# The last two feed forward layers of a Perceiver kernel: rotation on PSUM tiles, norms last, values behind the keys, token shift inside a projection

## The chip, the core and the metric

One core of one Trainium2 chip runs the whole program in one launch. The metric is the device time of an execution in microseconds (us). The profile is of one execution. TensorE's clock has two levels, 1.2 and 2.4 GHz; the profile gives the granted clock as a share of 2.4 GHz.

## What is computed

The reference is twelve residual blocks on x of 2 x 256 tokens by 256 channels. The change touches the twelfth, `L3_ffn`, which holds two layers (l = 0 and 1) of this form, each an attention with 8 heads of 64 and a gated feed forward:

```python
def _layer(x, wqkv, qs, ksc, wo, lg, lb, w1, b1, w2, b2):
    h = shift_token(x)                 # channels 128 to 255 one token later, per batch
    q, k, v = jnp.split(h @ wqkv, 3, axis=-1)
    q, k, v = (to_heads(q), to_heads(k), to_heads(v))
    q = l2norm(q) * qs                 # one norm per token and head
    k = l2norm(k) * ksc
    q, k = rotary_xpos(q, k)           # q*cos*scale + rotate_half(q)*sin*scale
    o = local_attention(q, k, v)
    x = x + o @ wo
    h = shift_token(x)
    h = layernorm(h) * lg + lb
    a, g = jnp.split(h @ w1 + b1, 2, axis=-1)
    x = x + (a * gelu(g)) @ w2 + b2
    return x
```

The block's own input is the layer norm of x; its output is added to x.

## The kernel before

The program is written out by hand, one function for each block and engine (`l3f_pe(l)`, `l3f_dve(l)`, `l3f_act(l)`, `l3f_pool(l)`, `l3f_sp(l)`), and each engine runs its functions in order. An event recorded with `at(...)` is a semaphore count; `wait_ge(engine, ...)` waits for it. `after(engine, stage)` waits for all engines' ends of a stage. Tokens lie in four tiles of 128 (t = 0 to 3, two of each batch). `banks` hands out the eight PSUM banks in turn; a bank is reused when the events given with `take` have come (`settle`).

A layer goes through these stages. The layer input XN is transposed on TensorE into HT (L289), and the second half of the channels is copied out one column further, which is the token shift (L2399). Queries and keys are projected, n = 0 to 7, four tiles of each, 512 wide (L318 through `tokp_pe`). ScalarE squares every tile into SQ (L2469), VectorE sums the squares by head (L2403). When all eight are there, one root (L2471) and one reciprocal (L2407) follow, and VectorE goes over the eight tiles again: scale by the norm out of PSUM (L2411), times q_scale or k_scale (L2418), the two halves of the turned part (L2424 and L2426, on GpSimd for odd n: L2506 and L2509), times the cosine table (L2434), sum (L2439). TensorE transposes the results (L2364), then projects the values (L318). The attention (`attn_pe` and the others) starts with L415. Its output OT3 goes through the output projection (L318, 16 matmuls of 256 columns) and is added to XN (L330). Then the shifted input XS of the layer norm is made: GpSimd copies the first half of the channels, and SP's queue moves the second half one partition down with two transfers per tile (L2534 to L2538). Statistics (L260, L262), root (L277) and scaling (L267, L269) of the four tiles follow, transposes (L289) and the affine step (L302). The feed forward is 24 matmuls of 512 columns (L310), Gelu (L2489), product (L2456), 24 matmuls of 256 (L318), the addition to XN (L330) and of b2 (L333). In layer 1 X is added (L2462) and stored (L2545). The block ahead, `l3a`, ends with a layer norm by tiles (`addout_dve` with `ln`), and has a fourth operand (L333) in each tile's addition. A ScalarE function table is loaded with `preload_act_table`. An f32 matmul is two records of TensorE in the profile, a transpose one.

## Time and profile before

| | us |
|---|---|
| three runs, median (lowest, highest) | 2343.68 (2337.89, 2343.77) |
| the profiled execution | 2344.69 |
| its span | 2343.4 |
| TensorE busy in the span | 2017.7 (86%) |
| VectorE busy | 1447.3 (62%) |
| ScalarE busy | 1161.7 (50%) |
| GpSimd busy | 555.7 (24%) |

The two layers take the last 290 us of the span: layer 0 from 2053.6, layer 1 from 2197.7. Busy shares are of the whole span; in the rows below the share of a stage is what counts. PE is TensorE, PEld its weight loads, DVE VectorE, ACT ScalarE, POOL GpSimd, SPq the queue of SyncE, PS PSUM, WK, WA and WB large SBUF tensors.

### The profile page before, as it was taken

The numbers are of one execution on the slowest core, as the hardware profiler recorded it, in microseconds if no ns is written. First come the engines' busy times: TensorE is split into PE (matmuls) and PEld (weight loads), VectorE is DVE, ScalarE is ACT, GpSimd is POOL, SyncE is SP. The second block draws the span as 40 slices with busy tenths as digits, with TensorE's granted clock in tenths as the row PEclk, the third lists the DMA queues.
The fourth block names the chain that finished last, engine by engine and source line by source line (L and its number), as shares of the span: only waits on it lengthen the run. The fifth ranks groups of instructions, "written<-read, shape, count | busy, mean of one in ns | idle before, by whom it ended". The sixth has DMA issues, their size and how long they took to land.

```text
span 2343.4 us, 36521 instructions
## 1 busy us (share of the span) xinstructions
PE 2017.7 (86%) x13415; PEld 1185.4 (51%) x13415; DVE 1447.3 (62%) x3518; ACT 1161.7 (50%) x2481; POOL 555.7 (24%) x849
## 2 busy tenths in 40 slices
PE   5999999998985899999998889988876877856776
PEld 2545554444553545554454655475555665624343
DVE  2577667784766377667784655412658994764462
ACT  2466666665433366566675611421527881613131
POOL 3132222213611322122200500000413441512030
PEclk8999999999987999999999989999988999978988
DMA  7455445560021655445541013520031322001100
GB/s 171 92 134 124 111 105 132 116 162 1 1 72 44 108 127 127 107 116 136 122 69 58 18 50 104 160 90 14 1 104 58 100 73 77 2 13 41 44 2 13
DMA packets 122546, 187.25 MB, mean 80 GB/s; under 512 B 22632, under 2 KB 70304, under 8 KB 122016
## 3 DMA queue, kind: packets, MB, share of 16 engines
q1 hardware_dynamic: 122368, 184.92, 31.8%
q8 instruction: 107, 1.75, 0.3%
q14 instruction: 71, 0.58, 0.1%
HBM read 131.86 MB, written 2.13 MB: 57 GB/s over the span
## 4 chain that ended last, share of the span: by engine, by line
PE 68%; DVE 16%; ACT 5%; SPq 4%; issue 2%; POOL 2%; DMA 2%; ACTq 0%; DVEq 0%; POOLq 0%
PE PS L712 9%; PE PS L694 9%; PE PS L663 8%; PE PS L310 7%; PE PS L318 6%; PE PS L630 5%; PE PS L618 4%; DVE WK L2108 3%; SPq L995 3%; PE PS L1637 2%; PE PS L1662 2%; PE PS L415 2%; PE PS L463 2%; PE PS L442 2%; ACT WK L514 2%
## 5 line engine op out<-in xcount | busy, mean ns | idle before, releaser
L768 DVE TENSOR_REDUCE WK<-PS 128x1 f32<-128x1024 f32 x512 | 609.2, 1221 | 310.4 <-PE PS L663 308.3
L874 ACT ACTIVATE WK<-PS 128x512 f32<-128x512 f32 x1024 | 542.0, 600 | 197.2 <-PE PS L694 191.2
L694 PE MATMUL PS<-WK 100*128 100x256 bf16 x2048 | 322.9, 275 | 7.1 <-ACT WK L874 6.4
L663 PE MATMUL PS<-WK 100*128 100x512 bf16 x1024 | 304.9, 381 | 8.7 <-DVE WK L768 3.7
L694 PEld LDWEIGHTS PS<-WK 100*128 100x128 bf16 x2048 | 166.8, 98 | 215.4 <-ACT WK L874 74.7
L712 PE MATMUL PS<-WK 128*32 128x256 f32 x3072 | 207.0, 386 | 0.0
L514 ACT ACTIVATE WK<-PS,WK 128x256 f32<-128x256 f32 (+1 forms) x320 | 140.6, 451 | 74.6 <-DVE WK L482 44.5
L540 POOL TENSOR_TENSOR WK<-WK 128x128 f32<-128x128 f32 (+1 forms) x128 | 65.0, 508 | 370.4 <-DVE WK L500 308.1
L936 POOL TENSOR_SCALAR WK<-WK 128x2 bf16<-128x2 f32 x64 | 12.5, 195 | 570.5 <-DVE WK L774 373.1
L712 PEld LDWEIGHTS PS<-WK 128*32 128x32 f32 x3072 | 80.6, 109 | 112.4 <-issue 78.0
L310 PE MATMUL PS<-HT,WB 128*128 128x512 f32 x248 | 120.8, 646 | 5.6 <-DVE HT L302 1.9
L544 POOL TENSOR_TENSOR WK<-WK 128x512 f32<-128x512 f32 x96 | 100.0, 1041 | 77.2 <-DVE WK L497 59.1
L923 POOL TENSOR_TENSOR WK<-WK 128x512 f32<-128x512 f32 x64 | 74.1, 1157 | 168.1 <-ACT WK L845 89.5
L663 PEld LDWEIGHTS PS<-WK 100*128 100x128 bf16 x1024 | 94.5, 98 | 36.9 <-DVE WK L768 16.2
L415 PE MATMUL PS<-WK 32*128 32x256 f32 (+2 forms) x640 | 85.8, 391 | 13.1 <-ACT WK L514 10.1
L491 DVE COPY WK<-PS 128x512 f32<-128x512 f32 (+1 forms) x144 | 88.3, 619 | 4.7 <-PE PS L442 4.7
L442 PE MATMUL PS<-idf,WK 128*128 128x128 f32 x576 | 84.5, 287 | 4.4 <-DVE WK L491 2.6
L310 PEld LDWEIGHTS PS<-HT,WB 128*128 128x128 f32 x248 | 51.2, 209 | 68.3 <-issue 60.3
L2108 DVE MAX8 WK<-WK 128x8 f32<-128x16 f32 x1088 | 84.5, 161 | 0.0
L442 PEld LDWEIGHTS PS<-idf,WK 128*128 128x128 f32 x576 | 66.7, 146 | 20.4 <-issue 9.3
L318 PE MATMUL PS<-WB,WK 128*128 128x256 f32 x320 | 71.2, 382 | 6.5 <-DVE WK L2456 3.3
L927 POOL TENSOR_TENSOR WK<-WK 128x512 bf16<-128x512 f32 x64 | 74.3, 1161 | 5.3
(334 smaller groups left out, 3303.9 us busy)
## 6 DMA issues: line engine op xcount, KB each, us to landing
WK<-WK SPq DMA_DIRECT2D x768, 64.0 KB
WB<-in_ctxT SPq DMA_DIRECT2D x78, 512.0 KB, 4.8
WK<-in_ctxT SPq DMA_DIRECT2D x40, 512.0 KB, 3.7
WA<-in_ctxT SPq DMA_DIRECT2D x26, 512.0 KB, 4.7
WK<-in_ctx SPq DMA_DIRECT2D x8, 1024.0 KB, 5.6
WK<-in_ctx SPq DMA_DIRECT2D x16, 512.0 KB, 3.9
WK<-scratch_q SPq DMA_DIRECT2D x12, 256.0 KB, 8.3
WB<-in_L3f_qkv SPq DMA_DIRECT2D x2, 1536.0 KB, 6.6
```

Source lines behind the costliest of these rows:

```text
L310: i = pe.e.matmul(b.ap, W[:, k, c0:c0 + 128], rhs[:, k, :], start=k == 0, stop=k == kt - 1)
L318: i = pe.e.matmul(b.ap[:, 0:n], lhs[:, k, t * 128:(t + 1) * 128], W[:, k, c0:c0 + n], start=k == 0, stop=k == kt - 1)
L415: x = pe.e.matmul(two[u].ap[:, c0:c1], qs[:, bb * 256 + q * 128:bb * 256 + (q + 1) * 128], ks[:, bb * 256:bb * 256 + c1 - c0], start=q == ...
L442: x = pe.e.transpose(b.ap[:, c:c + 128], PN[j % 4][:, q * 256 + kk * 128:q * 256 + (kk + 1) * 128], idf[:, :])
L514: ac.e.activation(PP[i % 4][:, c0:c1], tile[tag, "S", i][:, c0:c1], ACT.Exp, bias=r[:, q:q + 1], scale=1.0, accum_out=r[:, 2 + q:3 + q]).t ...
L630: x = pe.e.matmul(b.ap[:, t // 2, t % 2 * 256:t % 2 * 256 + 256], ct[:, k, t * 128:(t + 1) * 128], W["v"][:, k, :], start=k == 0, stop=k == 1)
L663: x = pe.e.matmul(b.ap[:, u, :], QS[0:100, h, bb * 256 + q * 128:bb * 256 + (q + 1) * 128], KS[s % 4][0:100, c * 1024 + u * 512:c * 1024 + ...
L694: x = pe.e.matmul(b.ap[:, j * 256:j * 256 + 256], KS[s % 4][0:100, kt * 128:(kt + 1) * 128], QS[0:100, h, bb * 256:bb * 256 + 256], start= ...
L712: x = pe.e.matmul(pv.ap[32 * j:32 * j + 32, 0:256], V[vbuf[g]][:, kt * 136 + 17 * hh:kt * 136 + 17 * hh + 32], PR[n % NPR][:, kt % 2 * 256 ...
L768: dv.e.tensor_reduce(mt[:, n:n + 1], tile["R", L, s, n].rearrange("p a b -> p (a b)"), AX, ALU.max).then_inc(*dv.at("R", L, s, n))
L874: ac.e.activation(PR[n % NPR], tile["S", L, s, i], ACT.Exp).then_inc(*ac.at("E", L, s, i))
L2108: dv.e.max(m8[:, g, :], n3[:, g, :]).then_inc(*dv.at())
```

## The change

- **Rotation.** The tables of cosine and sine are multiplied with q_scale and k_scale ahead of time, for both layers, on GpSimd in `l3a_pool` (`rope`); their loads move from layer 0's start to `l3x_sp`. VectorE multiplies each projected tile in PSUM with them, three products per tile, right behind its sum of squares. The halves are added on GpSimd for n = 0 to 5 and on VectorE for 6 and 7. The norm comes last: limit, root and reciprocal in two halves, the scaling of n = 0 to 3 on GpSimd and of 4 to 7 on VectorE.
- **Values** are projected behind the keys, ahead of the transposes. The attention waits for the transposed tiles pair by pair (`ready`).
- **Token shift.** The attention writes its output with a column of zeros ahead of each batch (OTP). XS is the shifted layer input, made at the layer's start; the output projection adds to it: channels 0 to 127 from the tokens as they are, 128 to 255 from columns one to the left. XN needs channels 128 to 255 unshifted too, which is a projection of its own (`o3r`, `rest(t)`): tiles 0 and 1 ahead of the layer norm's transposes, 2 and 3 behind them.
- **Layer norm** by tiles into XL, a tile behind the projection; the affine step's second half on ScalarE. ScalarE also takes the second copy of HT at the layer's start.
- **b2** is added on GpSimd ahead of the second product, in layer 1 also X; the store follows each tile's last addition. Layer 1's qkv and o weights are loaded once `o3r` has been projected.

VectorE, behind the last query and key tile of a layer. Before (the reductions, then all passes):

```order
L2403 TENSOR_REDUCE WK<-WK 128x8 x8
L2405 TENSOR_SCALAR WK<-WK 128x64
L2407 RECIPROCAL WK<-WK 128x64
L2411 TENSOR_TENSOR WK<-PS,WK 128x512 x8
L2418 TENSOR_TENSOR WK<-WK,WA 128x512
L2424 TENSOR_TENSOR WK<-WK,WA 128x8x32
L2426 TENSOR_TENSOR WK<-WK,WA 128x8x32
L2418 TENSOR_TENSOR WK<-WK,WA 128x512 x2
...
L2434 TENSOR_TENSOR WK<-WK,WA 128x512 x8
L2439 TENSOR_TENSOR WK<-WK 128x512 x8
L2442 COPY WK<-PS 128x512 x2
```

After (the last of eight rounds, and what follows):

```order
L2459 TENSOR_REDUCE WK<-WK 128x8
L2460 TENSOR_TENSOR WK<-PS,WK 128x512
L2462 TENSOR_TENSOR WK<-PS,WK 128x8x32
L2464 TENSOR_TENSOR WK<-PS,WK 128x8x32
L2445 TENSOR_SCALAR WK<-WK 128x32
L2473 TENSOR_TENSOR WK<-WK 128x512 x2
L2451 RECIPROCAL WK<-WK 128x32
L2480 TENSOR_TENSOR WK<-WK 128x512 x4
L2485 COPY WK<-PS 128x512 x4
L482 TENSOR_REDUCE WK<-PS 128x1 x4
```

The products moved into the rounds; one sum for two tiles and one scaling for four are left behind them, and the copies of transposed tiles went from two to four.

TensorE, from the projections to the attention, and from the output projection on. Before:

```order
L318 MATMUL PS<-WB,HT 128x512 x16
L2364 MATMUL PS<-idf,WK 128x128 x32
L318 MATMUL PS<-WB,HT 128x512 x8
...
L318 MATMUL PS<-WB,WK 128x256 x16
L289 MATMUL PS<-idf,WK 128x128 x8
L310 MATMUL PS<-HT,WB 128x512 x24
L318 MATMUL PS<-WB,WK 128x256 x24
```

After:

```order
L318 MATMUL PS<-WB,HT 128x512 x24
L2398 MATMUL PS<-idf,WK 128x128 x32
...
L2374 MATMUL PS<-WB,WK 128x128 x40
L289 MATMUL PS<-idf,WK 128x128 x8
L2374 MATMUL PS<-WB,WK 128x128 x8
L310 MATMUL PS<-HT,WB 128x512 x24
L318 MATMUL PS<-WB,WK 128x256 x24
```

The 8 values matmuls stand ahead of the transposes; the output projection has 32 matmuls of 128 columns and another 8 ahead of the layer norm's transposes, and 8 behind them.

VectorE, between output projection and second product. Before:

```order
L330 TENSOR_TENSOR XN<-PS,XN 128x256 x4
L260 BN_STATS st<-WK 128x6
L262 BN_AGGR mv<-st 128x2
...
L260 BN_STATS st<-WK 128x6
L262 BN_AGGR mv<-st 128x2
L267 RECIPROCAL rs<-rs 128x1
L269 TENSOR_SCALAR WK<-WK,mv,rs 128x256
...
L302 TENSOR_SCALAR HT<-PS,sm 128x512 x2
```

After:

```order
L2491 TENSOR_TENSOR WK<-PS,WK 128x256
L260 BN_STATS st<-WK 128x6
L262 BN_AGGR mv<-st 128x2
L267 RECIPROCAL rs<-rs 128x1
L269 TENSOR_SCALAR WK<-WK,mv,rs 128x256
...
L302 TENSOR_SCALAR HT<-PS,sm 128x512
L2501 TENSOR_TENSOR XN<-PS,XN 128x128 x4
L2506 SCALAR_TENSOR_TENSOR WK<-PS,sm,WK 128x512 x6
L330 TENSOR_TENSOR XN<-PS,XN 128x256 x4
```

The additions to XN left for one to XS in front of each tile's statistics; a half wide addition per tile stands behind the affine step, of which one half is left here.

The diff, cut to its core (GpSimd's and SP's rearranged loads and ScalarE's copies are told above):

```diff
+            sp.e.dma_start(tab, tiles(D["L3f_tab"])).then_inc(*d_tab.at())
+            for l in range(2):
+                for i, n in enumerate(("L3f_qs", "L3f_ks")):
+                    sp.e.dma_start(qks[l][i], D[n][l:l + 1, :].to_broadcast([128, 64])).then_inc(*d_tab.at())
...
+                    for c, s, n in ((0, 0, 64), (64, 32, 32), (96, 0, 32)):
+                        a = 128 * i + c
+                        po.wait_ge(po)
+                        po.e.tensor_tensor(rope[l][:, :, a:a + n], tab[:, :, a:a + n],
+                                           qks[l][i][:, s:s + n].rearrange("p (a d) -> p a d", a=1).to_broadcast([128, 4, n]),
+                                           ALU.mult).then_inc(*po.at("rope3", l))
...
+        OTP = WK[:, 16384:18440].rearrange("p (m b t) -> p m b t", m=4, b=2)
+        AF = [Attn(("af", l), 8, 2, 2, KT, VT, OTP, padded=True) for l in range(2)]
+
+
+                a = t % 2 * 128 + 1 - shift
+                for k in range(4):
+                    x = pe.e.matmul(tile[name][:, dst:dst + 128], OTP[:, k, t // 2, a:a + 128], W["o"][:, k, c:c + 128],
+                                    start=k == 0, stop=k == 3, skip_group_check=True)
+                return x
...
+            def rest(t):
+                proj(("o3r", l, t), t, 0, 128, 0, (dv, "o3r", l, t)).then_inc(*pe.at("o3r", l, t))
...
+            for t in range(NT):
+                tokp_pe(("v3", l, t), HT, 2, t, W["qkv"], 1024, 512, (ac, "v3", l, t))
...
+                        pe.wait_ge((po, dv)[which], "rot", l, which * 4 + t)
...
-            for t in range(NT):
-                tokp_pe(("v3", l, t), HT, 2, t, W["qkv"], 1024, 512, (ac, "v3", l, t))
...
+            def ready(k):
+                if k < 4:
+                    for which in range(2):
+                        pe.wait_ge((dv, ac)[k % 2], "qkt", l, which, k)
+                if k == 0:
+                    pe.wait_ge(ac, "v3", l, 3)
...
-            addout_pe(("o3f", l), OT3, 4, W["o"])
-            turn_pe(("hf", l), XS, (dv, ("lnf", l)), dv, dv)
+            for t in range(NT):
+                proj(("o3f", l, t), t, 0, 0, 0, (dv, ("o3f", l), t))
+                proj(("o3f", l, t), t, 128, 128, 1).then_inc(*pe.at("o3f", l, t))
+            for t in range(2):
+                rest(t)
+            turn_pe(("hf", l), XL, (dv, ("lnf", l)), dv, ac)
+            for t in range(2, NT):
+                rest(t)
...
+            def limit(i):
+                dv.wait_ge(dv)
+                dv.e.tensor_scalar(RN[:, 4 * i:4 * i + 4, :], RN[:, 4 * i:4 * i + 4, :], 1e-24, None, ALU.max).then_inc(
+                    *dv.at("limit", l, i))
...
+                dv.wait_ge(ac, "rn", l, i)
+                dv.e.reciprocal(RN[:, 4 * i:4 * i + 4, :], RN[:, 4 * i:4 * i + 4, :]).then_inc(*dv.at("inverse", l, i))
...
+                R = rope[l][:, n % 4, 128 * (n // 4):128 * (n // 4) + 128].rearrange("p (h d) -> p h d", h=1)
...
+                dv.e.tensor_reduce(RN[:, n, :], s3, AX, ALU.add).then_inc(*dv.at())
+                dv.e.tensor_tensor(q3[n], x3, R[:, :, 0:64].to_broadcast([128, 8, 64]), ALU.mult).then_inc(*dv.at())
+                dv.wait_ge(dv)
+                dv.e.tensor_tensor(s3[:, :, 0:32], x3[:, :, 32:64], R[:, :, 64:96].to_broadcast([128, 8, 32]),
+                                   ALU.mult).then_inc(*dv.at())
+                dv.e.tensor_tensor(s3[:, :, 32:64], x3[:, :, 0:32], R[:, :, 96:128].to_broadcast([128, 8, 32]),
+                                   ALU.mult).then_inc(*dv.at("qn", l, n))
+                if n == 3:
+                    limit(0)
+                if n == 5:
+                    invert(0)
+            limit(1)
+            for n in (6, 7):
+                dv.wait_ge(dv, "qn", l, n)
+                dv.e.tensor_tensor(q3[n], q3[n], SQ[n].rearrange("p (h d) -> p h d", d=64), ALU.add).then_inc(
+                    *dv.at("turned", l, n))
+            invert(1)
...
-                dv.e.tensor_tensor(q3[n], q3[n], qks[n // 4].rearrange("p (h d) -> p h d", h=1).to_broadcast([128, 8, 64]),
-                                   ALU.mult).then_inc(*dv.at("qs", l, n))
...
+                dv.e.tensor_tensor(q3[n], q3[n], RN[:, n, :].rearrange("p (h d) -> p h d", d=1).to_broadcast([128, 8, 64]),
+                                   ALU.mult).then_inc(*dv.at("rot", l, n))
             attn_dve(AF[l])
-            addout_dve(("o3f", l), XN)
             dv.wait_ge(d_shift[l])
             dv.wait_ge(po, "xs", l)
             for t in range(NT):
+                dv.wait_ge(pe, "o3f", l, t)
+                dv.e.tensor_tensor(XS[:, t, :], tile["o3f", l, t][:, 0:256], XS[:, t, :], ALU.add).then_inc(
+                    *dv.at(("o3f", l), t))
                 ln_a(("lnf", l), XS, t)
-            for t in range(NT):
-                ln_b(("lnf", l), XS, XS, t)
-            for f in range(2):
-                affine_dve(("hf", l), f, sm[:, 76:78], sm[:, 78:80])
+                if t:
+                    ln_b(("lnf", l), XS, XL, t - 1)
+            ln_b(("lnf", l), XS, XL, NT - 1)
+            dv.wait_ge(d_small[l])
+            affine_dve(("hf", l), 0, sm[:, 76:78], sm[:, 78:80])
...
+                dv.e.tensor_tensor(XN[:, t, 128:256], tile["o3r", l, t][:, 0:128], XN[:, t, 128:256], ALU.add).then_inc(
...
-            addout_dve(("o3w", l), XN, lambda t: b2row)
-            if l:
-                for t in range(NT):
-                    dv.wait_ge(dv, ("o3w", 1), "x", t)
-                    dv.e.tensor_tensor(X[:, t, :], X[:, t, :], XN[:, t, :], ALU.add).then_inc(*dv.at("out", t))
+            dv.wait_ge(po, "xb", l)
+            addout_dve(("o3w", l), X if l else XN)
...
+            ac.wait_ge(pe, ("hs", l), "T", 1, NT - 1)
+            ac.e.activation(HT[:, 1, :].rearrange("p (b t) -> p b t", b=2)[:, :, 1:256],
...
+                if n == 5:
+                    root(0)
+            for t in range(3):
+                value(t)
+            root(1)
             ac.e.preload_act_table(ACT.Exp)
...
+                po.e.tensor_scalar(XS[:, t, 0:128], XN[:, t, 0:128], 1.0, 1.0, ALU.mult, ALU.mult).then_inc(*po.at("xs", l))
+            for n in range(6):
+                q = QN[n // 4][:, n % 4, :]
+                po.wait_ge(dv, "qn", l, n)
-                                   ALU.mult).then_inc(*po.at("turned", l, n))
+                po.e.tensor_tensor(q, q, SQ[n], ALU.add).then_inc(*po.at("turned", l, n))
+            po.wait_ge(dv, "inverse", l, 0)
...
+                po.e.tensor_tensor(q3, q3, RN[:, n, :].rearrange("p (h d) -> p h d", d=1).to_broadcast([128, 8, 64]),
+                                   ALU.mult).then_inc(*po.at("rot", l, n))
...
+                po.e.tensor_scalar(XN[:, t, 0:128], XS[:, t, 0:128], 1.0, 1.0, ALU.mult, ALU.mult).then_inc(*po.at())
...
+                po.e.tensor_tensor(XN[:, t, :], XN[:, t, :], b2row, ALU.add).then_inc(*po.at("xb", l))
+                if l:
+                    po.wait_ge(po)
+                    po.e.tensor_tensor(X[:, t, :], X[:, t, :], XN[:, t, :], ALU.add).then_inc(*po.at("xb", l))
...
-                sp.wait_ge(dv, ("o3f", l), t)
+                sp.wait_ge(dv, "xl", l, t)
...
+                sp.wait_ge(pe, "o3r", 0, NT - 1)
...
-                    sp.wait_ge(dv, "out", t)
+                    sp.wait_ge(dv, ("o3w", 1), t)
```

## Rows read from the trace of the kernel before

**Rows 1.** Windows: start:end length, PE, PEld, DVE, ACT, POOL busy (count), PEclk, DMA.

```profile
2213.90:2239.00 25.10, 0.08 (x1) 0.11 (x1) 23.64 (x37) 3.39 (x4) 7.81 (x8) 0.55 0.00 0
...
2242.00:2245.40 3.40, 3.40 (x25) 3.40 (x24) 2.19 (x4) 2.29 (x5) 0.00 (x0) 0.76 0.00 0
...
2245.50:2252.40 6.90, 6.83 (x16) 2.66 (x14) 0.00 (x0) 2.59 (x6) 0.00 (x0) 1.00 0.00 0
2252.40:2279.40 27.00, 23.31 (x208) 15.36 (x208) 18.82 (x64) 16.86 (x73) 16.25 (x32) 1.00 0.01 2
...
2286.60:2303.10 16.50, 2.81 (x10) 1.55 (x9) 6.39 (x19) 2.46 (x5) 0.30 (x1) 0.65 0.04 12
...
2303.00:2306.00 3.00, 2.94 (x4) 1.42 (x5) 0.00 (x0) 0.00 (x0) 0.00 (x0) 0.50 0.00 0
...
2309.00:2312.00 3.00, 3.00 (x8) 1.33 (x8) 0.75 (x1) 0.69 (x1) 0.00 (x0) 1.00 0.00 0
```

**Rows 2.** The chain that ended last: start, length, engine, tile, line, count.

```profile
2138.25 7.19 PE PS L318 x32
...
2149.29 5.70 DMA WK<-XN
...
2162.13 22.34 PE PS L310 x48
...
2199.86 13.99 PE PS L318 x32
...
2279.44 7.19 PE PS L318 x32
...
2303.06 23.54 PE PS L310 x48
```

**Rows 3.** Timeline of VectorE and TensorE: start, length, operation, idle time before.

```profile
2060.51 0.69 DVE L2403 TENSOR_REDUCE WK<-WK 128x8 f32<-128x512 f32 x1 [4.27 <-ACT WK L2469]
...
2111.83 0.93 PE L415 MATMUL PS<-WK 64*128 64x128 f32 x8 [0.69 <-ACT WK L2481]
...
2202.56 0.69 DVE L2403 TENSOR_REDUCE WK<-WK 128x8 f32<-128x512 f32 x1 [2.81 <-ACT WK L2469]
...
2216.65 4.88 DVE L2411 TENSOR_TENSOR WK<-PS,WK 128x512 f32<-128x512 f32 x8
...
2222.16 0.42 DVE L2424 TENSOR_TENSOR WK<-WK,WA 128x256 f32<-128x256 f32 x1
2222.51 0.42 DVE L2426 TENSOR_TENSOR WK<-WK,WA 128x256 f32<-128x256 f32 x1
...
2253.02 0.93 PE L415 MATMUL PS<-WK 64*128 64x128 f32 x8 [0.69 <-ACT WK L2481]
```

**Rows 4.** VectorE and GpSimd side by side: timeline, and durations (min/median/max in ns).

```profile
1996.60 2.22 POOL L544 TENSOR_TENSOR WK<-WK 128x512 f32<-128x512 f32 x2 [19.65 <-DVE WK L497]
...
2223.61 1.10 POOL L2506 TENSOR_TENSOR WK<-WK,WA 128x256 f32<-128x256 f32 x1 [25.77 <-DVE WK L2418]
2224.16 0.83 DVE L2424 TENSOR_TENSOR WK<-WK,WA 128x256 f32<-128x256 f32 x1
...
L2424 DVE TENSOR_TENSOR WK<-WK,WA x8: 424/827/832, 2079.8 to 2230.0; 128x256 f32<-128x256 f32 x8
...
L2139 DVE TENSOR_REDUCE WK<-WK x17: 1219/1220/1222, 1760.9 to 1930.7; 128x4 f32<-128x1024 f32 x17
```

**Rows 5.** Groups of TensorE, matmuls with 16 columns at full clock.

```profile
L318 PE MATMUL PS<-WB,HT 128*128 128x16 f32 x16 | 1.9, 257 | 0.0
```

**Rows 6.** Timeline of VectorE, last tile of the previous block's layer norm.

```profile
2050.86 0.42 DVE L330 TENSOR_TENSOR X<-PS,X 128x256 f32<-128x256 f32 x1
...
2053.01 0.41 DVE L269 TENSOR_SCALAR XN<-X,mv,rs 128x256 f32<-128x256 f32 x1
```

**Rows 7.** Timeline of VectorE at the end of layer 1.

```profile
2338.88 0.42 DVE L330 TENSOR_TENSOR XN<-PS,XN 128x256 f32<-128x256 f32 x1 [1.71 <-PE PS L318]
...
2339.68 1.43 DVE L2462 TENSOR_TENSOR X<-X,XN 128x256 f32<-128x256 f32 x4
```

More of the change, by code:

```diff
@@ L2342, in build, with proj @@
         GG = [view(WK, 3072 + 512 * i, 512) for i in range(3)]
-        AF = [Attn(("af", l), 8, 2, 2, KT, VT, OT3) for l in range(2)]
+        OTP = WK[:, 16384:18440].rearrange("p (m b t) -> p m b t", m=4, b=2)
+        AF = [Attn(("af", l), 8, 2, 2, KT, VT, OTP, padded=True) for l in range(2)]
         def l3f_pe(l):
             W = W3[l]
+            def proj(name, t, dst, c, shift, *freed):
+                if freed:
+                    settle(take(banks, name, *freed))
+                a = t % 2 * 128 + 1 - shift
[5 more added lines that the diff above has]
+                proj(("o3r", l, t), t, 0, 128, 0, (dv, "o3r", l, t)).then_inc(*pe.at("o3r", l, t))
@@ L2394, in l3f_dve @@
                     dv.mark("xl", 0, t)
[L2395 to L2400 removed]
+            turn_dve(("hs", l), 0)
```

162 lines of the change are left out of this document (70 added, 92 removed).

## The prediction

> **What bounds the kernel now.** I read the stages of the last two layers first. In layer 1 TensorE has 0.08 us of work in 25.1 us while VectorE works 23.64 us of them: the norm and the rotation of queries and keys. After the attention comes a second stretch, 16.5 us with 2.81 us of TensorE work [rows 1]. Layer 0 repeats both. The chain of waits says what ends last in the second one: the output projection, then a transfer of 5.70 us into the shifted tile, then the layer norm [rows 2]. Around these two stretches everything hangs on TensorE. No other engine works on another stage meanwhile, so what is cut from the chain comes off the end, unless a new last wait stands in its place.
>
> **Rotation, before.** From the first reduction of squares to the first matmul of the attention: 2060.51 to 2111.83 = 51.3 us in layer 0, 2202.56 to 2253.02 = 50.5 us in layer 1 [rows 3]. It is serial: eight reductions at TensorE's pace, some 24 us of vector passes after the last of them, transposes, and last the value projection.
>
> **Rotation, after.** VectorE's work per tile moves under the projection. Per tile: a reduction (0.69 long, next start about 0.61 on), a 512 wide product out of PSUM (4.88 us for eight, 0.61 each), a wait for its own result (0.1), and two 256 wide products (0.42 long, the second 0.35 after the first) [rows 3]. 0.61 + 0.71 + 0.35 + 0.35 = 2.02 us. Eight make 16.2. The first limit and the first reciprocal stand among them (half as wide as now; 0.7 together, an estimate), so the loop is over 16.9 us after its start. TensorE gives a tile every 1.72 us and has three values tiles queued behind them; it doesn't bound this.
>
> GpSimd adds the halves of tiles 0 to 5 as they come and then scales the four query tiles. Two 512 wide operations take it 2.22 us [rows 4]; I use 1.15 for one with its gap. Tile 5 is ready at 12.4, its sum at 13.7, the four query tiles at 18.3 us after the start. VectorE's tail is, by the same 0.61 for 512 columns: two sums 1.25, four scalings 2.45, and by estimate limit 0.2 and reciprocal 0.35. Alone that would end at 21.1.
>
> Do the two engines hinder each other? Rows 4 say when: two SBUF inputs on VectorE and a GpSimd operation beside them take 0.83 us where 0.42 is the price alone, and the product ends 0.28 us after GpSimd's (2224.71, 2224.99). A reduction of one SBUF input is untouched (1219 to 1222 ns in 17 instances, GpSimd at work on a 1.9 us operation beside some of them). In the new loop the products have one input in PSUM, so I charge nothing there; in the tail both inputs are in SBUF, and I charge one GpSimd operation and a half, 1.5 us: 22.6. Then the transposes of tile 7's four blocks, and two query copies and a key copy, 512 wide (0.65 each) on VectorE: the attention starts at 24.7, and I take 25.2 for bank waits. Gains: 51.3 - 25.2 = **26.1**, 50.5 - 25.2 = **25.3**. Bounds: 23 (copies behind each other better than so) and 31 (the loop blocked too: six sums of up to 1.1 us).
>
> **Values.** Their 6.9 us lay between transposes and attention, and are now under VectorE's tail; that is contained in the 25.2. With them goes a cover: TensorE is idle before the key scalings end, and the transposes may run at the half clock, as they did (granted 0.76 in the last 3.4 us of them in layer 1, 0.14 us each [rows 1]). At 0.5 a transpose would take 0.21 instead of 0.11 us, and 16 of them 1.7 more; I take off **1.0** in each layer.
>
> **Token shift.** Before, from the output projection's first matmul to the feed forward's first: 2138.25 to 2162.13 = 23.9, 2279.44 to 2303.06 = 23.6 us [rows 2]. After, no transfer stands in it: the eight shift transfers and four copies run at the layer's start, some 60 us ahead of their use. TensorE now issues 128 column matmuls. The kernel has none with a full 128 row f32 weight that isn't a transpose. From below: 128 rows and 16 columns, 16 in 1.9 us, 0.12 each, so the load's own pace; 64 rows and 128 columns, 8 in 0.93 with the last one's tail of 0.18 or so, 0.11 each. From above: load and stream one after another, 0.22 [rows 3, 5]. I take 0.11, since the 256 column matmuls (32 in 7.19 us, 0.22 each) leave no room for a load outside the stream. 64 records make 7.1 us, as before. The last tile's sum, statistics, root and scaling: from 2050.86 to 2053.42 in the previous layer, which has one extra addition of 0.45: 2.1 us [rows 6]. That is 9.3; the transposes of the last tile and of the second half 0.7 more; then 16 records of two remaining tiles stand in TensorE's queue before the feed forward, 1.8 us. 11.9 in all. VectorE's affine of half 0 (0.8) and ScalarE's of half 1, with the Gelu table's load of 1.28 ahead of it, end by 10.7 and 11.0 and are under these 16. Gains: **12.0** and **11.7**; at 0.22 per record only about 1.5 each.
>
> **Clock.** The feed forward's 48 matmuls took 22.34 and 23.54 us [rows 2]: after the wait they start at half clock (granted 0.50 at 2303 to 2306 [rows 1]). The 32 of the first projection in layer 1, at full clock, took 13.99: 0.43 each and a tail of 0.59 [rows 2]; by that 48 take 20.8. TensorE no longer pauses for more than 1 us ahead of them: **1.5** and **2.7**; nothing if it stays cold.
>
> **Ends.** The bias is added on GpSimd, under the feed forward: 0.45 of layer 0's chain. In layer 1 the chain from the last product was an addition at 2338.88 and the last X addition ending at 2341.11 [rows 7]; now it ends with the first, 2339.30: **1.8**. Sum with layer 0's: **2.3**.
>
> **Costed at nothing.** Five more loads on SP before l3x's context loads (its first wait there is for TensorE); twelve products of the tables on GpSimd in l3a (2048 elements in each partition, so four times 1.11 and twelve gaps, 6 us), where it sat idle for 19.65 us before its first scaling [rows 4]; layer 1's weights, which wait for the last remaining projection but have 60 us; b2 and X additions on GpSimd in 20 us of feed forward; ScalarE's Sqrt table, which moves from behind the projection to layer 1's start, where it just meets the transposes.
>
> **Sum.** 26.1 + 25.3 - 2.0 + 12.0 + 11.7 + 4.2 + 2.3 = 79.6 us. The profiled execution took 2344.69 (span 2343.4), the median is 2343.68, 1 us less; so **2264 us**.
>
> **Rivals.**
> (1) *Loads are not hidden.* Weight loads wait for the matmul before them, and a 128 column record costs 0.22. 14.2 instead of 7.1 for the projection, and twice for the remaining parts (1.4 of the first two show behind the norm, 1.8 of the last two): 10 us more in each layer, 2284. Against it stand the 256 column rows above. The Trainium skill ("TensorE: Matmul & The Clock Gate", Part 3) says that a load overlaps only with matmuls of another row group, which would give this; the trace speaks against it, with full-row f32 loads of 0.19 beside a start every 0.22 us. Chance 0.08.
> (2) *Contention.* GpSimd's ten operations block VectorE's PSUM products also, or are themselves blocked, 4 to 6 us per layer: about 2274. Against it: the unaffected rows of one SBUF input. Chance 0.12.
> (3) *Slower: the clock does not come back.* Before, real matmuls (the values) came between transposes and attention, and the attention ran wholly at 1.00 [rows 1]. Now it follows transposes and a pause. If TensorE stays at 1.2 GHz through attention, projection and first feed forward product, their 23.3 + 7.2 + 20.8 = 51 us in a layer double: 2264 + 103 = 2367. It turns slower than before once three quarters of that work is at the half clock. Against it: in layer 1's feed forward the full clock is back within 6 us of dense work (0.50 at 2303 to 2306, 1.00 at 2309 to 2312 [rows 1]). Chance 0.03, a third of it for a partial fall that leaves no change. The Trainium skill ("TensorE: Matmul & The Clock Gate", Part 4) says that transposes don't lift the clock; here the trace differs: it was granted 0.76 during transposes, and 1.00 from the first values matmul on.
> (4) *It does not do what it says*: some wait keeps rotation behind the projection, as when banks are freed late. The four values tiles take the banks of query tiles 0 to 3, freed 8 us earlier; so only a late transpose is at stake. All but the rotation's 49.4 us stays, 30 us: 2314. Chance 0.03.
>
> **How the numbers follow.** My forecast has 0.74, its own range 2255 to 2272 (bounds 23 for the rotation, clock terms at nothing or in full). With (2) and half of (1) the range is **2255 to 2280**. A measurement tells 0.3%, 7 us: faster by more than that 0.97 (the forecast, (1), (2) and (4)), within it 0.01, slower 0.02 (both from (3)).
>
> **What would show it.** Right: the first attention matmul 24 to 26 us after the first reduction; no VectorE product from PSUM over 0.70 us while GpSimd works; output projection records at 0.11; its start to the feed forward's in 12 us; the feed forward at 20.8 in both layers. Wrong: GpSimd operations of over 1.3 us in the loop, a query scaling that ends later than VectorE's last, or a granted clock under 1.00 behind the first 6 us of the attention.

## The result

The changed kernel took **2263.62 us** (median of 4 runs, 2255.93 to 2266.04), the kernel before 2343.72 (2337.89 to 2344.42) on the same chip: a ratio of 0.9658, 95% interval 0.963 to 0.9686. The forecast was 2264, its range 2255 to 2280. Two later measurements of the same kernel gave 2259.35 against 2344.23, ratio 0.9643 [0.9622, 0.9664], and 2258.54 against 2342.89, ratio 0.964 [0.9619, 0.9661]; all 13 runs of it lie between 2255.11 and 2266.04, with a median of 2259.35. So the change is worth some 84 us, and the 80.1 of the first measurement, which the forecast met almost to the digit, was a small sample on its high side. The traces say the same. From the first transpose of layer 0 to the end of the program they show 2053.57 to 2343.4 = 289.8 us before and 2049.14 to 2254.5 = 205.4 us after: 84.4 us. (As a whole these two executions differ by 88.9 us, for the changed one also reached the two layers 4.4 us earlier. The stages ahead of them scatter by more than that, as shown further down.) The forecast's sum was 79.6. Four of its terms were too careful and one too hopeful. One of the four, the slow transposes, was no question of size: what it feared didn't happen.

The chain that ended last, in the trace of the changed kernel (start, length, engine, tile, line, count; it answers to [rows 2]):

```profile
2106.92 7.43 PE PS L2374 x64
2119.09 20.62 PE PS L310 x48
2141.33 10.64 PE PS L318 x48
2207.25 7.43 PE PS L2374 x64
2219.43 20.62 PE PS L310 x48
2241.66 10.64 PE PS L318 x48
```

The transfer of 5.70 us is gone from it, the output projection is 64 records of 128 columns (32 matmuls, two records each) in 7.43 us, 0.116 each, the feed forward starts 12.17 and 12.18 us after the output projection, and its 48 records take 20.62 in both layers.

VectorE, GpSimd and TensorE at the end of layer 1's projection (timeline: start, length, engine, line, operation, idle time before; it answers to [rows 3]). The first five lines are one round of the new loop, beginning with the first reduction:

```profile
2157.09 0.69 DVE L2459 TENSOR_REDUCE WK<-WK 128x8 f32<-128x512 f32 x1 [3.15 <-ACT WK L2531]
2157.70 0.68 DVE L2460 TENSOR_TENSOR WK<-PS,WK 128x512 f32<-128x512 f32 x1
2158.41 0.42 DVE L2462 TENSOR_TENSOR WK<-PS,WK 128x256 f32<-128x256 f32 x1
2158.75 0.41 DVE L2464 TENSOR_TENSOR WK<-PS,WK 128x256 f32<-128x256 f32 x1
2159.09 0.68 DVE L2459 TENSOR_REDUCE WK<-WK 128x8 f32<-128x512 f32 x1
...
2173.03 0.41 DVE L2464 TENSOR_TENSOR WK<-PS,WK 128x256 f32<-128x256 f32 x1
2173.48 0.62 DVE L2445 TENSOR_SCALAR WK<-WK 128x32 f32<-128x32 f32 x1
2174.01 2.13 DVE L2473 TENSOR_TENSOR WK<-WK 128x512 f32<-128x512 f32 x2
2176.07 0.34 DVE L2451 RECIPROCAL WK<-WK 128x32 f32<-128x32 f32 x1
2176.44 2.50 DVE L2480 TENSOR_TENSOR WK<-WK 128x512 f32<-128x512 f32 x4
2178.86 2.48 DVE L2485 COPY WK<-PS 128x512 f32<-128x512 f32 x4
...
2169.36 1.27 POOL L2575 TENSOR_TENSOR WK<-WK 128x512 f32<-128x512 f32 x1 [0.70 <-DVE WK L2464]
2170.78 4.82 POOL L2580 TENSOR_TENSOR WK<-WK 128x512 f32<-128x512 f32 x4
...
2175.15 2.43 PE L2398 MATMUL PS<-idf,WK 128*128 128x128 f32 x17
...
2179.00 1.64 PE L2398 MATMUL PS<-idf,WK 128*128 128x128 f32 x13 [0.27 <-DVE WK L2480]
2180.84 0.93 PE L419 MATMUL PS<-WK 64*128 64x128 f32 x8 [0.20 <-DVE WK L2485]
```

A round takes 2.00 us (2157.09 to 2159.09). The attention starts 2180.84 - 2157.09 = 23.75 us after the first reduction; in layer 0 it is 2056.31 to 2080.51 = 24.2. TensorE goes from the last values matmul straight into 17 transposes: the query's 16 and the first of the keys, whose tiles were scaled by then. It waits only for the scalings of the last key tiles, three times for 0.2 to 0.3 us.

TensorE's clock in the stretches that [rows 1] show for before in layer 1 (window, its length, PE busy, granted clock), here of layer 0: the transposes, the attention, projection to feed forward, and the feed forward:

```profile
2075.00:2080.40 5.40, 4.55 (x33) 1.00 0.02 3
2080.50:2106.90 26.40, 23.31 (x208) 1.00 0.01 1
2106.90:2119.00 12.10, 11.98 (x105) 1.00 0.01 1
2119.00:2141.30 22.30, 20.69 (x49) 1.00 0.26 95
```

It stays at its higher level (2.4 GHz) in all of them, and in the same stretches of layer 1 (2175.00 to 2241.60) as well, where before it stood at 0.76 in the last transposes and at 0.50 when the feed forward began.

### The profile page after: what moved, and what is told of

Its sections match the earlier page's. It is cut to its first block, busy times and chain, and to the rows that moved or that the text cites. A ratio compares the mean times of both kernels' runs of the same rounds, so it can differ in the third digit from the quotient of the medians.

```text
span 2254.5 us, 36833 instructions
## 1 busy us (share of the span) xinstructions
PE 2012.7 (89%) x13543; PEld 1189.8 (53%) x13543; DVE 1423.1 (63%) x3498; ACT 1162.5 (52%) x2483; POOL 581.0 (26%) x887
## 3 DMA queue, kind: packets, MB, share of 16 engines
HBM read 131.86 MB, written 2.13 MB: 59 GB/s over the span
## 4 chain that ended last, share of the span: by engine, by line
PE 70%; DVE 17%; ACT 4%; SPq 3%; issue 2%; POOL 2%; DMA 2%; ACTq 0%; DVEq 0%; POOLq 0%
PE PS L716 10%; PE PS L698 10%; PE PS L667 9%; PE PS L310 7%; PE PS L634 5%; PE PS L622 4%; PE PS L318 4%; DVE WK L2112 3%; PE PS L1641 3%; PE PS L1666 3%; SPq L999 2%; PE PS L419 2%; PE PS L467 2%; PE PS L446 2%; ACT WK L518 2%
## 5 line engine op out<-in xcount | busy, mean ns | idle before, releaser
L878 ACT ACTIVATE WK<-PS 128x512 f32<-128x512 f32 x1024 | 542.3, 601 | 198.5 <-PE PS L698 192.5
L310 PE MATMUL PS<-HT,WB 128*128 128x512 f32 x248 | 114.9, 620 | 3.6 <-ACT HT L298 1.6
L667 PEld LDWEIGHTS PS<-WK 100*128 100x128 bf16 x1024 | 95.0, 98 | 33.9 <-DVE WK L772 16.1
L863 ACT ACTIVATE WK<-PS 128x512 f32<-128x512 f32 x48 | 26.9, 596 | 96.2 <-PE PS L634 96.2
```

What stands on the lines that cost most here:

```text
L310: i = pe.e.matmul(b.ap, W[:, k, c0:c0 + 128], rhs[:, k, :], start=k == 0, stop=k == kt - 1)
L667: x = pe.e.matmul(b.ap[:, u, :], QS[0:100, h, bb * 256 + q * 128:bb * 256 + (q + 1) * 128], KS[s % 4][0:100, c * 1024 + u * 512:c * 1024 + ...
L878: ac.e.activation(PR[n % NPR], tile["S", L, s, i], ACT.Exp).then_inc(*ac.at("E", L, s, i))
```

## Experiments

### Each half of the change alone

The first keeps the new rotation and values order, and takes the output projection, the transfers behind it, the norm and the additions of b2 and X from the kernel before:

```diff
-            for t in range(NT):
-                proj(("o3f", l, t), t, 0, 0, 0, (dv, ("o3f", l), t))
-                proj(("o3f", l, t), t, 128, 128, 1).then_inc(*pe.at("o3f", l, t))
...
-            turn_pe(("hf", l), XL, (dv, ("lnf", l)), dv, ac)
...
+            addout_pe(("o3f", l), OT3, 4, W["o"])
+            turn_pe(("hf", l), XS, (dv, ("lnf", l)), dv, dv)
...
+                sp.wait_ge(dv, ("o3f", l), t)
+                sp.e.dma_start(XS[1:128, t, 128:256], XN[0:127, t, 128:256]).then_inc(*d_shift[l].at())
```

The second is the reverse, the kernel before, rotation and values order with it, and those parts of the change put in:

```diff
-            addout_pe(("o3f", l), OT3, 4, W["o"])
-            turn_pe(("hf", l), XS, (dv, ("lnf", l)), dv, dv)
+            for t in range(NT):
+                proj(("o3f", l, t), t, 0, 0, 0, (dv, ("o3f", l), t))
+                proj(("o3f", l, t), t, 128, 128, 1).then_inc(*pe.at("o3f", l, t))
...
-                sp.wait_ge(dv, ("o3f", l), t)
+                sp.wait_ge(dv, "xl", l, t)
```

> Rotation on PSUM tiles, norms last and values behind the keys as in the changed kernel; everything behind the attention as before (shift by transfers between output projection and layer norm, norms in two passes, b2 and X on VectorE). My terms behind the attention were 12.0 + 11.7 for the shift, 4.2 for the clock, 2.3 for the ends: so 30 us over the changed kernel, 2294, and 50 under before. The feed forward's 48 matmuls should be back at 22.3 to 23.5 us, since TensorE pauses ahead of them again. Rival (terms overlap, the shift's gain needs the rotation's full clock): under 2285.

> The other half: the layer up to the attention as before, all behind it as in the changed kernel. Expected 2343.7 - 30.2 = 2313.5; with the first kernel of this call the two gains should add up to the whole 80 us. Output projection to feed forward 12.2 us, feed forward 20.6 us. Rival (parts share a wait): the two gains together are under 70 or over 90 us.

The rotation alone took 2297.71 us (2293.05 to 2306.01), ratio 0.9806 [0.9774, 0.9838]; the rest alone 2314.26 (2310.96 to 2317.7), 0.9873 [0.9845, 0.9901]. From layer 0's first transpose to the end the traces show 2056.54 to 2291.7 = 235.2 and 2056.78 to 2316.4 = 259.6 us. Against 289.8 these are gains of 54.6 and 30.2, in sum 84.8, and both together gave 84.4: in the traces **the parts add up**, and neither lives on the other. The medians of four runs each say it less sharply: 46.0 and 29.5 us, 75.5 in sum, with the rotation's runs spread over 13 us and its traced run the fastest of them. That the whole gain is more than either half's is clear of the noise; that the sum is exact is read from one trace of each. The chain of the rotation alone, then that of the rest alone:

```profile
2113.50 7.19 PE PS L318 x32
2124.46 5.71 DMA WK<-XN
2137.30 22.52 PE PS L310 x48
...
2251.43 23.48 PE PS L310 x48
```

```profile
2141.46 7.43 PE PS L2361 x64
2153.64 20.62 PE PS L311 x48
...
2281.28 20.62 PE PS L311 x48
```

The feed forward is slow (22.52, 23.48) exactly where the transfer and its wait stand ahead of it, and 20.62 where they don't: the clock term belongs to this half of the change, the token shift with its norm by tiles, and not to the rotation.

### Values behind the transposes again

```diff
-            for t in range(NT):
-                tokp_pe(("v3", l, t), HT, 2, t, W["qkv"], 1024, 512, (ac, "v3", l, t))
...
+            for t in range(NT):
+                tokp_pe(("v3", l, t), HT, 2, t, W["qkv"], 1024, 512, (ac, "v3", l, t))
```

Between the two places stand the transposes. ScalarE's copies of the values are moved likewise.

> Changed kernel with the value projection back behind the transposes. Its 6.9 us then lie on the path again, with 0.3 us for the last copy: 7.2 per layer, 2278. If the pause of TensorE ahead of the transposes also drops its clock, 33 transposes take up to 3.5 us more in part hidden by the key scalings: up to 2282. Rival (values were never on the path once rotation is early): 2264.

2278.91 us (2272.66 to 2282.44), ratio 0.9719 [0.9691, 0.9748]. In the trace 2057.08 to 2277.9 = 220.8 us, 15.4 more than the first trace of the changed kernel and 16.3 more than its two later ones (204.5; where these 0.9 come from stands under "All together"). TensorE's timeline in layer 0, VectorE's last scalings, then TensorE's clock in the transposes:

```profile
2078.74 0.30 PE L2396 MATMUL PS<-idf,WK 128*128 128x128 f32 x1 [3.52 <-POOL WK L2579]
...
2082.43 5.39 PE L2396 MATMUL PS<-idf,WK 128*128 128x128 f32 x29 [1.06 <-POOL WK L2579]
...
2087.66 7.03 PE L318 MATMUL PS<-WB,HT 128*128 128x512 f32 x16
2095.47 0.93 PE L419 MATMUL PS<-WK 64*128 64x128 f32 x8 [0.78 <-ACT WK L2527]
...
2083.21 2.50 DVE L2480 TENSOR_TENSOR WK<-WK 128x512 f32<-128x512 f32 x4
```

```profile
2082.00:2083.50 1.50, 1.07 (x5) 0.50 0.00 0
...
2085.00:2086.50 1.50, 1.50 (x9) 0.50 0.00 0
2086.50:2087.60 1.10, 1.10 (x12) 0.96 0.06 15
```

So the order pays mainly by the 7.03 us of values, and by 0.6 for the copy of the last values tile, for which the attention waits 0.78 us here and 0.20 for its own copy in the changed kernel. The transposes do run at the half clock after a pause of 3.52 us: here 29 take 5.39 us; in the changed kernel 17 take 2.43 and 13 take 1.64, 0.14 and 0.13 each. But most of that lies beside VectorE's key scalings and costs nothing. From the end of the last scaling (2083.21 + 2.50 = 2085.71) to the first values matmul it is 1.95 us, where the changed kernel's last transpose ends 1.70 us behind its last scaling: 0.25 us. In layer 1 it is 2.44 us, so 0.7.

### All rotation work on VectorE

GpSimd's six sums and four scalings are done by VectorE behind its loop:

```diff
-            for n in (6, 7):
+            for n in range(8):
...
-            for n in range(4, 8):
-                if n < 6:
-                    dv.wait_ge(po, "turned", l, n)
+            for n in range(8):
```

> Changed kernel with GpSimd's six sums and four scalings of each layer moved to VectorE's tail. VectorE: ten operations of 0.61 us more, 6.1, less the 1.3 us that it lost to GpSimd in the tail (0.43 before the limit, 0.85 in the two sums): 4.8 per layer, 2273. Rival (contention: GpSimd holds VectorE up as much as it helps): 2264 or less, and VectorE's PSUM products shorter than 0.68 and 0.42 us.

2270.71 us (2268.07 to 2270.97), ratio 0.9688 [0.9659, 0.9716]; in the trace 216.8 us for the two layers, 11.4 more than the first trace of the changed kernel and 12.3 more than the later ones, where 9.6 were expected. Groups of VectorE in layer 0 (line, operation, tiles, shapes, count | busy us, mean ns of one | idle), first with GpSimd at work, the changed kernel:

```profile
L2460 DVE TENSOR_TENSOR WK<-PS,WK 128x512 f32<-128x512 f32 x8 | 5.4, 680 | 0.0
...
L2473 DVE TENSOR_TENSOR WK<-WK 128x512 f32<-128x512 f32 x2 | 2.1, 1103 | 0.0
...
L2445 DVE TENSOR_SCALAR WK<-WK 128x32 f32<-128x32 f32 x2 | 0.8, 396 | 0.1
```

and with GpSimd idle, the experiment:

```profile
L2460 DVE TENSOR_TENSOR WK<-PS,WK 128x512 f32<-128x512 f32 x8 | 5.4, 679 | 0.0
...
L2473 DVE TENSOR_TENSOR WK<-WK 128x512 f32<-128x512 f32 x8 | 4.9, 684 | 0.0
...
L2445 DVE TENSOR_SCALAR WK<-WK 128x32 f32<-128x32 f32 x2 | 0.4, 181 | 0.1
```

This is rival (2) put to the test. A product with one input in PSUM takes 680 ns beside GpSimd and 679 without it: **no contention**. A sum with both inputs in SBUF takes 1103 against 684, and the small limit 396 against 181 (a mean of two: 0.18 us for the one with GpSimd idle, 0.61 for the one beside a scaling). The blocking that [rows 4] showed is there, and where the prediction put it. What remains above the 9.6 is the clock: TensorE waits 4.29 us here before its first transpose, 31 transposes take 7.16 us, and the attention starts 3.5 us behind the last scaling (2083.31 to 2086.84; 3.1 in layer 1) where the changed kernel has 1.9.

### The layer norm by steps

In this one each step of the norm is done for all four tiles, as before, instead of tile by tile; all else is as changed. It is the norm between output projection and feed forward. The expectation below puts it behind the feed forward, which is a slip, and prices it there.

```diff
-                if t:
-                    ln_b(("lnf", l), XS, XL, t - 1)
-            ln_b(("lnf", l), XS, XL, NT - 1)
+            for t in range(NT):
+                ln_b(("lnf", l), XS, XL, t)
```

> Layer norm behind the feed forwards is done by steps (each step for all four tiles) as in the kernel before, the rest as changed. Theory: the last transpose of a layer waits for no more than the last tile's own steps when the norm goes by tiles; by steps 1.6 to 2 us per layer come back in the one layer that is followed by another, and as much at the end of the kernel: 2267 us. Rival: the last tile is what counts either way, since its sums come last: 2264 us, no change.

2265.98 us (2260.09 to 2269.75), ratio 0.9668 [0.9645, 0.9691], where the changed kernel, measured beside it, took 2259.35. The time is near the 2267 expected, but only because that was reckoned from 2263.6: the difference is 6.6 us where 3.4 were expected. The two intervals of the ratio overlap, so by the medians alone even that is not sure. In the trace the two layers take 2051.19 to 2267.9 = 216.7 us against the changed kernel's 204.5 in its second trace (2049.07 to 2253.6). The stretch behind the output projection, TensorE's timeline and clock:

```profile
2120.11 0.33 PE L289 MATMUL PS<-idf,WK 128*128 128x128 f32 x1 [1.94 <-DVE WK L269]
...
2122.79 3.62 PE L2374 MATMUL PS<-WB,WK 128*128 128x128 f32 x16
```

```profile
2120.20:2126.20 6.00, 5.72 (x24) 0.52 0.00 0
```

The wait itself grows to 1.94 us, as expected of a norm whose last tile comes late. What was not expected: TensorE's clock is at its lower level after it (0.52; 16 records in 3.62 us, 1.95 in the changed kernel). So the start of the output projection to that of the second product grows from 34.41 to 40.18 us in layer 0 and to 40.04 in layer 1, 5.8 and 5.6 and not 1.6 to 2. (The other 0.8 lies mostly in layer 0's first projection, which the edit doesn't touch.) This small edit of the change carries more than its own steps, since it spares TensorE the pause. Why the median moved by only 6.6 us is not settled. Its five runs are 2260.1, 2261.5, 2266.0, 2269.5 and 2269.8, and the trace is of the run with 2269.5; that the two low ones kept the clock in a layer would fit, but there is no trace of them.

### The remaining parts behind the feed forward's first half

```diff
             turn_pe(("hf", l), XL, (dv, ("lnf", l)), dv, ac)
-            for t in range(2, NT):
-                rest(t)
...
+            for t in range(2, NT):
+                rest(t)
```

> The first product's remaining parts on token tiles 2 and 3 are issued behind the 24 matmuls of the feed forwards that need only tiles 0 and 1. Theory: in the changed kernel these remaining parts take 1.79 us on the chain in each of the two layers while TensorE later pauses for the second product; moved there, about 1.0 to 1.2 us per layer leave the chain, the stretch from the output projection to the first feed forward is 10.4 us instead of 12.2, and the time is 2261 us. Rival: the work only changes places on TensorE, since no pause takes it up: 2263.6, no change.

2261.06 us (2255.97 to 2262.1), ratio 0.9643 [0.9623, 0.9664]: no difference that could be told from the changed kernel. The trace shows a small one. Its chain and TensorE's timeline, and one line of ScalarE's timeline in the changed kernel:

```profile
2113.09 7.43 PE PS L2374 x64
2124.50 20.84 PE PS L310 x48
...
2146.97 10.63 PE L318 MATMUL PS<-WB,WK 128*128 128x256 f32 x48
```

```profile
2117.40 0.78 ACT L2548 ACTIVATE HT<-PS,sm 128x512 f32<-128x512 f32 x1 [0.30 <-PE PS L289]
```

Output projection to feed forward is 11.41 us instead of 12.17 and not less: in the changed kernel the 16 remaining records had covered ScalarE's half of the affine step, which ends 11.3 us after the projection's start (2118.18 - 2106.92), and TensorE now waits 1.02 us. The profile puts this wait to VectorE's two additions to XN (L2501), but they end at 2124.36, as does ScalarE's half, and of the two the code makes the feed forward's first matmul wait only for the latter. TensorE's second product starts 33.9 us after the output projection instead of 34.4. That is 0.5 per layer, half of what was expected, and far inside the scatter.

### Upstream: GpSimd's twelve products, and layer 3's first attention

> GpSimd's twelve products of the rotary table (7.37 us) are issued behind its part of layer 3's first attention instead of ahead of it. Theory: GpSimd is idle 12.22 us there in any case, so they are hidden where they stand: 2263.6 us, no change, attention 51.1 us. Rival: they share VectorE's memory port and hold up the projection's tail there: up to 3 us faster, 2260.6 us.

```diff
+            attn_pool(A3)
...
-            attn_pool(A3)
```

The products stand between the two places. 2257.78 us (2253.15 to 2259.87), ratio 0.9631 [0.9609, 0.9654], and layer 3's first attention takes 51.11 us, against 51.08 in the changed kernel's second trace: no change, as costed.

> The changed kernel once more, for its spread and a second trace. In its first trace layer 3's first attention took 55.6 us (1984.28 to 2039.87) with TensorE granted 0.50 from 1990 to 2002, where before and three experiments took 51.1. Theory: that is scatter from execution to execution and not a cost of the change; then this trace shows about 51.1 us there with the two last layers at 205.4 us again, and the median is 2256 to 2266 us. Rival: it belongs to the changed program; then 55.6 us again.

This was asked because the first trace of the changed kernel had a stage that the change doesn't touch and that took 4.5 us longer: layer 3's first attention, 1984.28 to 2039.87 = 55.6 us, against 1993.18 to 2044.30 = 51.1 before. The second trace shows 1988.72 to 2039.80 = 51.1 with the same program, so it is **scatter from execution to execution**, and no fixed cost of the change. TensorE waits there once for 1.34 us for ScalarE. Its timeline from this wait on, in the first trace of the changed kernel, then in the second:

```profile
1988.46 1.89 PE L419 MATMUL PS<-WK 32*128 32x256 f32 x8 [1.34 <-ACT WK L518]
...
1992.53 2.08 PE L419 MATMUL PS<-WK 32*128 32x256 f32 x8
```

```profile
1992.91 1.80 PE L419 MATMUL PS<-WK 32*128 32x256 f32 x8 [1.34 <-ACT WK L518]
...
1996.80 1.13 PE L419 MATMUL PS<-WK 32*128 32x256 f32 x8
```

The same pause in both; after it one execution has eight matmuls still at 2.08 us, the other back at 1.13. Of twelve traces of kernels that pause there, this attention took 55.6 us in three (the first of the changed kernel, and those of the two sections before this one) and 51.1 in nine, the one trace of the kernel before among them. Whether the long form is as frequent in the kernel before, one trace can't say.

> Six matmuls of 512 bf16 columns into an unused PSUM bank are put into TensorE's queue at the third token tile of layer 3's first attention, where it pauses for 1.34 us and where its granted clock then stays at 0.50 for about 12 us in some executions (that attention takes 55.6 us in three traces of the changed kernel or of a variant, 51.1 us in the others). They compute nothing that is used. Theory: the pause drops the clock, so with it filled the attention takes 51.1 us or less in the trace and the median falls by about half of 4.5 us: 2258 us. Rival: the added work (about 1.5 us) delays the attention by itself and the clock falls elsewhere: 2262 us, and 52 us or more for the attention.

```diff
+            def fill(k):
+                if k == 2:
+                    for event in bank[7].owner:
+                        pe.wait_ge(*event)
+                    for i in range(6):
+                        x = pe.e.matmul(bank[7].ap[:, 0:512], idb[:, :], msk[:, 1, :], start=True, stop=True,
+                                        skip_group_check=True)
+                    x.then_inc(*pe.at(tag, "fill"))
```

2258.71 us (2256.22 to 2259.66), ratio 0.9635 [0.9615, 0.9656], and the changed kernel measured beside it 2258.54 (2257.39 to 2261.1). A window of this kernel at the place (length, PE busy, granted clock), and one of the changed kernel's second trace behind its pause:

```profile
1993.00:1996.00 3.00, 2.95 (x19) 1.00 0.00 0
```

```profile
1993.00:1996.00 3.00, 3.00 (x15) 0.54 0.00 0
```

With the pause filled the clock does not fall, here and in the one other kernel that fills it, where it fell in all twelve that don't: so the fall hangs on the pause, though the filling also adds dense work, and the two weren't tried apart. But the attention takes 51.07 us, just as in the executions in which the clock came back soon, so some 3 us at the lower level cost it nothing, and TensorE doesn't set its pace there; and layer 0's first projection, 22.25 us after a short attention, took 23.9 here (2055.11 to 2079.02). The trace of the two layers is 205.95 us, 1.4 more. No gain shows, in the median or in the spread.

### All together

> The remaining parts of token tiles 2 and 3 behind the 24 feed forward matmuls (0.55 us per layer in the trace of that change alone), and GpSimd's products of the rotary table behind its part of the attention (nothing in the trace). Theory: 1.1 us less than the changed kernel in the two last layers, 204.3 us from the first transpose to the end against 204.5 to 205.4, and a median of 2259 us that the scatter hides. Rival: the two disturb one another in the feed forwards' queues: 2262 us or more.

> The two edits of the kernel above and the six filling matmuls together. Theory: the gains add, 2255 to 2257 us median, with 51.1 us or less for layer 3's first attention. Rival: the filling costs what it gives: 2260 us.

> The changed kernel a third time, as the measure for the three kernels of this call: 2256 to 2264 us. Theory: the two last layers take 204.5 to 205.4 us in every trace, and what differs from execution to execution is layer 3's first attention, 51.1 or 55.6 us, and stages ahead of it. Rival: the two last layers scatter as well, by over 2 us.

Medians 2257.2 (2254.93 to 2259.33), 2255.94 (2254.91 to 2257.7) and 2258.54 (2257.39 to 2261.1), ratios 0.9633 [0.9612, 0.9654], 0.9628 [0.9608, 0.9649] and 0.964 [0.9619, 0.9661]. From layer 0's first transpose to the end: 203.5, 203.5 and 204.5 us. The 1.0 us of the remaining parts shows in both traces; the times can't tell the three apart. That attention took 51.1 us in all three. The changed kernel's two layers took 205.4, 204.5 and 204.5 us in its three traces: they don't scatter by 2 us, the stages ahead of them do: layer 3's first attention starts at 1984.28, 1988.72 and 1991.63 us in them. The 0.9 between 205.4 and 204.5 lies in layer 0's first projection. It starts at the half clock in each of them, but took 23.36 us in the first trace and 22.25 and 22.24 in the others. In the other traces that have these 48 records in a row it is 23.4 behind a long attention and 22.2 to 22.3 us behind a short one (but 23.9 in the trace noted above). Why, no run here shows.

## Why the prediction was right, and where its terms were off

Each term, as the sum had it and as the first pair of traces shows it:

| Term | Predicted | Measured | Off by |
|---|---|---|---|
| rotation, layers 0 and 1 | 26.1 + 25.3 | 51.3 - 24.2 = 27.1; 50.5 - 23.75 = 26.7 | +2.4 |
| allowance for cold transposes | -2.0 | 0 (contained in the line above) | +2.0 |
| output projection to feed forward | 12.0 + 11.7 | 23.88 - 12.17 = 11.7; 23.62 - 12.18 = 11.4 | -0.6 |
| feed forward at the higher clock | 1.5 + 2.7 | 22.34 - 20.62 = 1.7; 23.54 - 20.62 = 2.9 | +0.4 |
| ends and what is left | 2.3 | 84.4 less the above = 2.9 | +0.6 |
| sum | 79.6 | 84.4 | +4.8 |

**Bound.** Both stretches read off [rows 1, 2] were on the path, and no other engine became late in their place: each half alone gave its share in the traces. Of the signs named for being right, the first matmul of layer 1's attention lies a little under its 24 to 26 us (23.75); none of the signs of being wrong came up.

**Loop.** The forecast had 2.02 us for a round and 16.9 us for the loop; it was 1.98 to 2.00, and 2157.09 to 2173.44 = 16.4. The step "the products have one input in PSUM, so I charge nothing there" is shown by the groups with and without GpSimd. GpSimd's sums took 1.27 us and not 1.15. I had priced them by a product with a broadcast input [rows 4], 1.04 us without its gap; its four scalings, which have one, took 1.15 each here (4.82 in all). Whether a full second input or VectorE's work beside it makes up the difference wasn't tried. It cost nothing, as GpSimd was idle 0.70 us ahead of every sum.

**Tail.** "One GpSimd operation and a half, 1.5 us" was nearly it. In layer 1 the limit took 0.62 instead of 0.18 and the two sums 2.13 instead of some 1.3, 1.3 in all. The scalings ended 2176.44 + 2.50 - 2157.09 = 21.85 us after the start (forecast 22.6), and the attention began 1.9 behind them, where the forecast had 2.1 and another 0.5 for bank waits that did not come.

**The term whose condition failed: cold transposes.** The text said that "TensorE is idle before the key scalings end, and the transposes may run at the half clock", and took off 2.0. It was sized from the old order, where a pause of 25 us stood ahead of the transposes. It overlooked that with the values in front and the query tiles scaled by GpSimd, 17 transposes are ready when the values end, so TensorE has no pause ahead of the transposes, and the granted clock is 1.00 through all of them. The two experiments that make a pause (3.52 and 4.29 us) got the slow transposes. What they paid is of the size allowed: 0.25 and 0.7 us with the values last, where most of the slow ones ran beside the key scalings, 1.6 and 1.2 with all work on VectorE, where more of them came behind the last scaling. So the price was sound and the condition for it was not.

**Does the clock come back without real matmuls?** Rival (3) hung on this. The windows of the experiment with the values last answer it: TensorE ran nothing but transposes from 2078.74 on, at 0.50 from 2082.00 to 2086.50, and then at 0.96 in the last 1.1 us of them; the attention and all behind it kept 1.00. The Trainium skill ("TensorE: Matmul & The Clock Gate", Part 4) says that the clock's higher level doesn't engage for transposes in TensorE's transpose mode. In this trace it rose while these f32 `transpose` instructions alone ran. They are one record each where an f32 matmul has two; whether they use the mode that the page means, no run here shows. In the changed kernel the question never arose.

**Weight loads.** 64 records of 128 columns, each with a weight load of its own, took 7.43 us, 0.116 each, against 0.22 by rival (1). The Trainium skill ("TensorE: Matmul & The Clock Gate", Part 3), by which a load overlaps only with matmuls of another row group, would have given that rival's 2284 us; the trace disagrees for full 128 row f32 weights. (The same part of the page also lets a load run ahead when it goes to the background buffer, which would fit the trace.)

**Token shift.** Predicted 11.9, measured 12.2 in both layers. The parts as written, 7.1 + 2.1 + 0.7 + 1.8, add up to 11.7 and not 11.9, which hid some of the miss. The norm's last tile was scaled 9.56 us after the projection's start (forecast 9.3) and its transposes ended at 10.2 (10.0). The affine steps were under the 16 remaining records as said: with these moved away, a wait came up in their place.

**Layer norm by tiles** was part of the 11.9 and priced there as work on the last tile only. Its larger part is that TensorE doesn't pause there (11.98 us busy of 12.10): with the norm by steps, projection to second product was 5.8 and 5.6 us longer.

**Ends.** From the second product to the next layer's first transpose it is 11.65 us before and 11.19 after, 0.45 as said; from layer 1's second product to the end of the program 2328.22 to 2343.4 = 15.2 and 2241.66 to 2254.5 = 12.8, so 2.3 us where 1.8 were expected. The sum had counted up to the last addition, where 1.8 is right; what follows it, the last store, took 2.3 us before (2341.11 to 2343.4) and 1.8 after (2252.74 to 2254.5).

**Upstream at nothing.** Right as far as the runs go: it made no difference where GpSimd's products stand, and the first trace's longer attention was scatter.

**The size of the miss.** The sum was 4.8 us short, and the first measurement's median lay 4.6 us above that of the nine later runs of the same kernel (2259.03). The two nearly cancelled. That the forecast agreed within 0.4 us is luck; that it was within 5 is not.

## What to carry to other kernels

Where one engine waits while another does elementwise work, move that work under the matmuls that feed it, tile by tile, and let the second elementwise engine take operations whose inputs are in SBUF, while the first reads PSUM: here its products from PSUM were not slowed beside GpSimd (680 and 679 ns), and its sums of two SBUF inputs were (1103 and 684). Order TensorE's queue so that something independent lies right ahead of each wait: the time of that work is saved (7.03 us per layer here), and where the pause would be followed by work on the path, so is the lower clock behind it. Price a step of 1 or 2 us that shortens a TensorE pause with the matmuls behind it at both clock levels, and judge gains of a few microseconds by one stage in the trace, since the medians of four or five runs scatter by 4.

## What was not expected of the hardware

A pause of 1.34 us in light work (matmuls with 32 rows) was followed by the lower clock in all twelve executions that have it, but for very different stretches. In each the granted clock fell within the first microsecond behind the pause. It was back at 1.00 four microseconds behind it in nine of them, and only fourteen behind it in the other three, with the code of that stage the same. A 1.94 us pause behind 80 dense records brought the clock down in the norm experiment; the one of 1.63 us ahead of the second product did not in any trace that has it, with 10.6 us for its 48 records each time. Filling the pause of 1.34 us with matmuls that nobody uses kept the clock at 1.00, and bought nothing, since TensorE was not the bound there.
